# Three products of split operands for the local q, k and v in a two-branch transformer kernel

## Time and profile before

| | |
|---|---|
| median of 3 runs | 3817.17 us (3813.94 to 3817.77) |
| profiled execution | 3824.69 us, its span 3822.8 us |
| mean granted TensorE clock | 0.966 |
| TensorE busy | 3278.0 us, 86% |
| VectorE, ScalarE, GpSimd busy | 55%, 44%, 26% |

### The profile page before, as it was taken

How to read it: one execution, slowest core, us unless ns; L and a number is a source line. 1 busy time by engine, 2 the same in 40 slices (tenths; PEclk the granted TensorE clock), 3 DMA queues, 4 the chain that set the end, 5 groups by cost and what they waited for, 6 DMA issues and landing times.

```text
span 3822.8 us, 96024 instructions
## 1 busy us (share of the span) xinstructions
PE 3278.0 (86%) x35300; PEld 2174.9 (57%) x35300; DVE 2101.3 (55%) x7233; ACT 1694.2 (44%) x3181; POOL 983.3 (26%) x743
## 2 busy tenths in 40 slices
PE   1689898898989889898988989889898988979898
PEld 0356465565656556465655646566565655656565
DVE  2365564646556464654647556464655646465464
ACT  1245354444535354453544535344453534445354
POOL 2141230403223041321404133140412304132140
PEclk9799999999999999999999999999999999999999
DMA  3000000000000000000000000000000000000000
GB/s 79 1 7 2 10 2 10 2 2 10 2 10 2 10 2 2 10 2 10 2 5 7 2 10 2 10 2 2 10 2 10 2 10 2 2 7 2 7 2 4
DMA packets 42627, 26.49 MB, mean 7 GB/s; under 512 B 13266, under 2 KB 40828, under 8 KB 42108
## 3 DMA queue, kind: packets, MB, share of 16 engines
q1 hardware_dynamic: 42108, 19.59, 1.8%
HBM read 14.96 MB, written 4.19 MB: 5 GB/s over the span
## 4 chain that ended last, share of the span: by engine, by line
issue 43%; PE 28%; DVE 16%; POOL 6%; ACT 4%; SPq 1%; DMA 0%; DVEq 0%; POOLq 0%; ACTq 0%; PEldq 0%
PE bank L1093 4%; PE bank L1179 3%; DVE ss L925 3%; PE bank L1136 3%; POOL rnorm L652 3%; DVE scratch L920 3%; PE bank L1011 3%; PE bank L1122 2%; PE bank L1194 2%; DVE scratch L922 2%; DVE bank L865 2%; ACT scratch L757 2%; DVE scratch L923 2%; PE bank L1114 1%; DVE bank L880 1%
## 5 line engine op out<-in xcount | busy, mean ns | idle before, releaser
L652 POOL TENSOR_TENSOR rnorm<-ssc,minus_half 128x8 f32<-128x8 f32 x264 | 484.7, 1836 | 997.1 <-DVE ssc L927 994.6
L865 DVE CUSTOM_DVE_ANT_0 bank<-bank,future 128x128 f32<-128x128 f32 (+3 forms) x1024 | 467.0, 527 | 145.6 <-PE bank L1055 143.6
L880 DVE CUSTOM_DVE_ANT_0 bank<-bank,band 128x192 f32<-128x192 f32 x1056 | 341.3, 394 | 277.2 <-PE bank L1074 265.7
L723 ACT ACTIVATE probs<-bank 128x512 f32<-128x512 f32 (+1 forms) x768 | 347.0, 530 | 205.4 <-PE bank L1101 205.2
L1093 PE MATMUL bank<-Qa,Ka 64*128 64x512 f32 (+3 forms) x2048 | 395.1, 465 | 44.5 <-DVE ss L925 36.5
L1136 PEld LDWEIGHTS bank<-Va,probs 128*64 128x64 f32 x10240 | 338.8, 144 | 117.2 <-issue 107.4
L757 ACT ACTIVATE scratch<-bank 128x512 f32<-128x512 f32 x264 | 158.7, 601 | 512.0 <-DVE ss L925 286.1
L1136 PE MATMUL bank<-Va,probs 128*64 128x65 f32 x10240 | 375.2, 231 | 0.7
L641 POOL TENSOR_TENSOR lrstd<-lvar,minus_half 128x4 f32<-128x4 f32 x33 | 33.4, 1013 | 1308.1 <-DVE lvar L943 1308.1
L1179 PE MATMUL bank<-Lqkv,resid 128*128 128x512 f32 x528 | 289.2, 674 | 32.6 <-ACT resid L746 23.5
L731 ACT ACTIVATE lprobs<-bank 128x384 f32<-128x384 f32 x528 | 226.8, 491 | 199.0 <-PE bank L1124 195.5
(11 more groups left out here) (144 smaller groups left out, 7148.9 us busy)
## 6 DMA issues: line engine op xcount, KB each, us to landing
x_res<-in_L_attn_x SPq DMA_DIRECT2D x16, 256.0 KB, 2.9
x_rows<-in_L_attn_x SPq DMA_DIRECT2D x16, 256.0 KB, 3.1
out<-yT SPq DMA_DIRECT2D x16, 256.0 KB, 2.7
Lqkv<-in_L_ffn_wqkv SPq DMA_DIRECT2D x2, 768.0 KB
yT<-in_L_attn_W_qkv SPq DMA_DIRECT2D x6, 256.0 KB, 2.7
rope_t<-in_rope SPq DMA_DIRECT2D x8, 128.0 KB
Lw<-in_L_ffn_w SPq DMA_DIRECT2D x2, 341.0 KB
Lwo<-in_L_ffn_wo SPq DMA_DIRECT2D x2, 256.0 KB
```

The source lines that it names most:

```text
L652: g.tensor_tensor(rnorm[s][:, :], ssc[s][:, :], minus_half[:, :], ALU.pow).then_inc(rnorm_ready.sem, 1)
L723: psum.raise_read(a.activation(probs[j][:, at:at + n], psum.bank(task, (u, j))[:, 0:n], ACT.Exp, scale=float(HEAD) ** -0.5), task, (u, j))
L865: ins = v.tensor_tensor_reduce(psum.bank(task, (u, j))[:, at:at + n], psum.bank(task, (u, j))[:, at:at + n], future[:, SEQ - n:SEQ], 1.0, ...
L880: ins = v.tensor_tensor_reduce(psum.bank(task, (u, j))[:, k * BAND:(k + 1) * BAND], psum.bank(task, (u, j))[:, k * BAND:(k + 1) * BAND], b ...
```

## The change

The weights `Lqkv[l]` become a pair of a high and a low part, made once at the start. A new step `f_split` per layer makes the same pair `hT` of the layer's input (ScalarE copies the high part, VectorE subtracts), and `f_qk` and `f_v` use `product` with it. `h` goes away: the norm writes over `x_res`, and so SP loads `x_res` later, after the transposes `xt`, and behind the load of `x_rows`. The loads of all four weight thirds or halves that are split go to tiles that the loop uses later (`ff`, `GLU`, `Kf[1]`, `Qf[1]`), without a wait between them. The mask image `outside` loses an unused third. The planner has the new step, its needs, and new prices for `f_qk` and `f_v`, and so it gives a new order.

In the new order `a_neg.0` stands ahead of `f_qk.0.0`; `f_st.0.0` stands ten steps behind `f_neg.0.0`; the end of a turn reads `a_pv.7.1, f_ot.1.3, a_ot.7, f_wo.1, a_out.7, a_end, xt, f_down.0, f_mean.1, f_var.1, f_rep.1, f_gate.1, f_up.1.*, f_down.1, out`. Before it read `f_wo.1, a_out.6, a_pv.7.0, f_down.0, a_pv.7.1, f_mean.1, a_ot.7, f_var.1, a_out.7, a_end, xt, f_rep.1, f_gate.1, f_up.1.*, f_down.1, out`.

```diff
-    "f_qk": (0.9, [("act", 1.2, 0.0), ("dve", 5.2, 0.6), ("pool", 7.0, 2.9)], 2),
-    "f_v": (0.45, [("act", 0.6, 0.0)], 1),
+    "f_split": (0.0, [("act", 0.65, 0.0), ("dve", 0.7, 0.65)], 0),
+    "f_qk": (1.45, [("act", 1.2, 0.0), ("dve", 5.2, 0.6), ("pool", 7.0, 2.9)], 2),
+    "f_v": (0.72, [("act", 0.6, 0.0)], 1),
...
-    return start + [(kind, l, t) for kind, t in F_FRONT] + rounds(F_ROUND, LPAIRS, (l,)) + [("f_wo", l)]
+    return start + [("f_split", l)] + [(kind, l, t) for kind, t in F_FRONT] + rounds(F_ROUND, LPAIRS, (l,)) + [("f_wo", l)]
...
-        "f_qk": lambda: [("f_qk", 0, TILES - 1)] if at[0] else [("f_first",)],
-        "f_v": lambda: [] if at[0] else [("f_first",)],
+        "f_split": lambda: [("f_qk", 0, TILES - 1), ("f_v", 0, TILES - 1)] if at[0] else [("f_first",)],
+        "f_qk": lambda: [("f_split", at[0])],
+        "f_v": lambda: [("f_split", at[0])],
...
-        Lqkv = [sb(f"Lqkv{l}", [P, 3 * INNER]) for l in range(DEPTH)]
+        Lqkv = [[sb(f"Lqkv{l}_{s}", [P, 3 * INNER], F32R) for s in ("hi", "lo")] for l in range(DEPTH)]
-        outside = sb("outside", [P, 2, 3, BAND], BF16)
+        outside = sb("outside", [P, 2, 2 * BAND], BF16)
-        h = sb("h", [P, TILES, DIM])
+        hT = [sb(f"hT_{s}", [P, SEQ], F32R) for s in ("hi", "lo")]
...
+        PIECE = 3 * INNER
+        raw = [sem(f"raw{k}") for k in range(DEPTH + 2)]
+        staging = [part[:, 0:3].rearrange("p c n -> p (c n)") for part in (ff, GLU, Kf[1], Qf[1])]
+        split_parts = [(raw[k], staging[k][:, n * SEQ:(n + 1) * SEQ], [part[:, at + n * SEQ:at + (n + 1) * SEQ] for part in w])
+                       for k, (w, at) in enumerate([(Lqkv[0], 0), (Lqkv[1], 0), (Wqkv, 0), (Wqkv, PIECE)]) for n in range(PIECE // SEQ)]
...
-            for k in range(WPIECES):
-                if k:
-                    sp.wait_ge(split_lo, k)
-                sp.dma_start(yT[:, :], W_qkv[:, k * SEQ:(k + 1) * SEQ]).then_inc(staged, 16)
+            for k, part in enumerate(staging[DEPTH:]):
+                sp.dma_start(part, W_qkv[:, k * PIECE:(k + 1) * PIECE]).then_inc(raw[DEPTH + k], 16)
...
-                sp.wait_ge(norm_ready.sem, norm_ready.now(i, ("norm",), "n"))
+                psum.wait_read(sp, i, ("out",), "t", True)
+                sp.sem_inc(carried["sp"], 1)
+                load(x_rows[:, :, :], bass.ds(i, 1), x_again)
+                psum.wait_filled(sp, i, ("xt",), "x")
                 sp.sem_inc(carried["sp"], 1)
                 if last:
                     sp.sem_inc(x_loaded, 16)
                 else:
                     load(x_res[:, :, :], bass.ds(i + 2, 1), x_loaded)
-                psum.wait_read(sp, i, ("out",), "t", True)
-                sp.sem_inc(carried["sp"], 1)
-                load(x_rows[:, :, :], bass.ds(i, 1), x_again)
...
+                    elif kind == "f_split":
+                        l = task[1]
+                        if l == 0:
+                            psum.wait_read(act, i, ("f_first",), "h")
+                        else:
+                            psum.wait_read(act, i, ("f_down", 0), "w", True)
+                        act.sem_inc(carried["act"], 1)
+                        psum.wait_filled(act, i, ("f_v", 1 - l, TILES - 1), "v", l == 0)
+                        act.sem_inc(carried["act"], 1)
+                        a.activation(hT[0][:, :], resid[l][:, 0:SEQ], ACT.Copy).then_inc(hi_ready.sem, 1)
...
-                    ins = v.tensor_scalar(h[:, t, :], src[:, t, :], mv[:, t, 0:1], rstd[:, t:t + 1],
+                    ins = v.tensor_scalar(src[:, t, :], src[:, t, :], mv[:, t, 0:1], rstd[:, t:t + 1],
...
+                    elif kind == "f_split":
+                        l = task[1]
+                        dve.wait_ge(hi_ready.sem, hi_ready.now(i, task, "h"))
+                        v.tensor_tensor(hT[1][:, :], resid[l][:, 0:SEQ], hT[0][:, :].bitcast(F32),
+                                        ALU.subtract).then_inc(lo_ready.sem, 1)
...
-                            psum.raise_filled(mm(bank[:, :], resid[l][:, tile(t)], Lqkv[l][:, c * INNER:(c + 1) * INNER], start=True,
-                                                 stop=True), task, m)
+                            psum.raise_filled(product(bank[:, :], [part[:, tile(t)] for part in hT],
+                                                      [w[:, c * INNER:(c + 1) * INNER] for w in Lqkv[l]]), task, m)
```

More of the change, by code:

```diff
@@ L212, in in_order @@
     return at == sorted(at)
-assert in_order(("norm",), ("f_first",), ("f_qk", 1, 0), ("f_wo", 0), ("f_wo", 1), ("f_down", 0), ("f_mean", 1), ("out",))
+assert in_order(("norm",), ("f_first",), ("f_split", 1), ("f_qk", 1, 0), ("f_wo", 0), ("f_wo", 1), ("f_down", 0), ("f_mean", 1), ("out",))
 assert in_order(("norm",), ("f_first",), ("xt",)) and in_order(("a_proj", PAIRS - 1), ("xt",))
@@ L481, in prenorm_attention_and_local_transformer @@
         clip_ready = Signal(sem("clip_ready"), dict(f_qk="qk"))
+        hi_ready = Signal(sem("hi_ready"), dict(f_split="h"))
+        lo_ready = Signal(sem("lo_ready"), dict(f_split="l"))
         norm_ready = Signal(sem("norm_ready"), dict(norm="saen"))
@@ L557, in _ @@
                         sp.dma_start(dst[rows, k, :], src[of, :]).then_inc(halved, 16)
[L558 removed]
+                    sp.dma_start(outside[rows, k, :], band[of, 1:3, :].rearrange("p a n -> p (a n)")).then_inc(halved, 16)
             weights(1)
[L560 to L563 removed]
+            for k, part in enumerate(staging[DEPTH:]):
+                sp.dma_start(part, W_qkv[:, k * PIECE:(k + 1) * PIECE]).then_inc(raw[DEPTH + k], 16)
             sp.dma_start(Wout[:, :, :], W_out.rearrange("(c p) n -> p c n", p=P)).then_inc(whole[1], 16)
             sp.sem_inc(stored, 16)
[L566 removed]
+            psum.wait_filled(sp, -1, ("xt",), "x")
             load(x_res[:, :, :], slice(1, 2), x_loaded)
             def sequence(i, last):
[L571 removed]
+                psum.wait_read(sp, i, ("out",), "t", True)
+                sp.sem_inc(carried["sp"], 1)
+                load(x_rows[:, :, :], bass.ds(i, 1), x_again)
+                psum.wait_filled(sp, i, ("xt",), "x")
                 sp.sem_inc(carried["sp"], 1)
@@ L672, in _ @@
             act.wait_ge(params, PARAMS)
-            for k in range(WPIECES):
-                act.wait_ge(staged, 16 * (k + 1))
-                a.activation(Wqkv[0][:, k * SEQ:(k + 1) * SEQ], yT[:, :], ACT.Copy).then_inc(split_hi, 1)
+            for loaded, src, (hi, lo) in split_parts:
+                act.wait_ge(loaded, 16)
+                a.activation(hi, src, ACT.Copy).then_inc(split_hi, 1)
+            act.wait_ge(split_lo, len(split_parts))
             def alone(i, task, mark, dst, src, func=ACT.Copy, **kw):
@@ L809, in _ @@
                                     scales[:, l, kind:kind + 1, :].broadcast_to([P, TILES, HEAD]), ALU.mult).then_inc(tables, 1)
-            for k in range(WPIECES):
+            for k, (loaded, src, (hi, lo)) in enumerate(split_parts):
                 dve.wait_ge(split_hi, k + 1)
                 dve.sem_inc(carried["dve"], 1)
[L813 to L816, removed]
+                dve.wait_ge(loaded, 16)
+                v.tensor_tensor(lo, src, hi.bitcast(F32), ALU.subtract).then_inc(split_lo, 1)
+            dve.wait_ge(split_lo, len(split_parts))
             dve.wait_ge(tables, 4 * DEPTH)
@@ L1000, in _ @@
             pe.wait_ge(whole[0], WHOLE[0])
+            pe.wait_ge(split_lo, 3 * INNER // SEQ)
             def product(dst, left, right):
@@ L1025, in steps @@
                         pe.wait_ge(norm_ready.sem, norm_ready.now(i, ("norm",), "n"))
-                        transposes(i, task, "x", lambda t: h[:, t, :])
+                        transposes(i, task, "x", lambda t: x_res[:, t, :])
                     elif kind == "a_proj":
@@ L1114, in steps @@
                                     mm(bank[j][:, 0:2 * BAND], row_of[HALF[j], k, :],
-                                       outside[HALF[j], k, 1:3, :].rearrange("p a n -> p (a n)"), start=(k == 0), stop=False)
+                                       outside[HALF[j], k, :], start=(k == 0), stop=False)
                             for k in range(2):
@@ L1167, in steps @@
                         pe.wait_ge(norm_ready.sem, norm_ready.now(i, ("norm",), "n"))
-                        transposes(i, task, "h", lambda t: h[:, t, :])
+                        transposes(i, task, "h", lambda t: x_res[:, t, :])
                     elif kind == "f_qk":
@@ L1171, in steps @@
                         if t == 0:
-                            if l == 0:
-                                psum.wait_read(pe, i, ("f_first",), "h")
-                            else:
-                                psum.wait_read(pe, i, ("f_down", 0), "w", True)
+                            pe.wait_ge(lo_ready.sem, lo_ready.now(i, ("f_split", l), "l"))
                             pe.sem_inc(carried["pe"], 1)
@@ L1183, in steps @@
                         bank = psum.claim(pe, i, task, "v")
```

(6 more changed lines are left out.)

12 lines of the change are left out of this document (5 added, 7 removed).

## The result

The changed kernel takes 3916.4 us (median of 4 runs, 3910.6 to 3922.0) against 3817.0 of the kernel before (3813.9 to 3817.8): ratio 1.026, interval 1.024 to 1.027. It is slower, as predicted, but by 99 us and not 33; 3916 lies outside the range of 3770 to 3905. The profiled execution has a span of 3920.1 us and a mean granted clock of 0.928, before 3822.8 and 0.966.

What follows compares the result with a forecast made beforehand. TensorE's queue, 86% busy, was taken as the bound. A turn: -3.3 products, +0.7 middle, +1.3 head, +4.5 tail = +3.2; sixteen turns +51, start -18, so +33 us: 3850, range 3770 to 3905.

Steps and rivals of the forecast that it cites:

- The products' passes: q, k, v products as three passes each instead of float32: gain of 3.3 us a turn, ends 2.6 and 4.1.
- rival (c): q, k, v passes cost three quarters of the old, 2.1 us a turn better: 3816, no change; chance 0.11.
- The middle: Middle of the turn: bank waits grow, other waits go in the new order; +0.7 us a turn, ends -3 and +4.
- the count: TensorE work missing between a k product and the seventh bank after, per tile: total 8.9 to 12.6 us a turn.
- The head: Start of a turn: f_split.0's copy and subtraction in series delay f_qk.0.0; +1.3 us a turn, ends 0 and 2.6.
- The tail: f_down.0 to f_gate.1 with no other work left between: 3.8 us a turn bare, up to 7.1 with clock; 4.5 taken.
- the three new waits: Sign in the tail: waits of 1.2 to 1.6 us ahead of f_mean.1, f_var.1 and f_rep.1, sixteen of each.
- The clock: Lower clock priced only in the tail, between 3.8 and 7.1 us a turn; no clock term for head or middle.
- rival (b): Tail runs at the low clock as in the first sequence, 7.1 instead of 4.5 us a turn: 3892; chance 0.16.
- first pass: First layer-0 pass, ahead of the loop: f_split adds 1.4, four product pairs give back about 0.5 each; -0.6 us.
- The start: W_qkv loads issued at once ahead of the first norm, which moves from 66.2 to near 49: gain of 17 us.
- Rival (a): Steps moved from the tail cover the middle's waits, -3 there, -2.0 us a turn in all: 3767; chance 0.28.

Runs made afterwards that it cites:

- e11: Changed kernel in the old order, without the split step (q, k, v from wrong tokens), plus 33 zero-weight products a turn: 3785.0 us, ratio 0.991.
- e9: Kernel before with only the new loading of W_qkv at the start, plus 33 zero-weight products a turn ahead of eight waiting steps: 3791.9 us, ratio 0.993.
- e3: Changed kernel with the last steps of a turn in the old order, other work again between the tail's steps: 3870.7 us, ratio 1.014.
- e5: Changed kernel with three unused bf16 products added at each of five waits of the tail: 3936.3 us, ratio 1.030.
- e8: Changed kernel with 38 zero-weight products a turn ahead of ten waiting steps of the head and middle: 3868.0 us, ratio 1.012.
- e4: Kernel before with only the start changed, both halves of W_qkv loaded at once to tiles not used yet: 3803.5 us, ratio 0.996.
- e7: Kernel before with only the split step added, awaited by TensorE, products still float32: 3886.2 us, ratio 1.018.

## Why the prediction was half right

**The products' passes: right, at the upper end.** Timeline after, q, k and v of one tile at full clock:

```profile
1175.79 0.50 PE L1025 MATMUL bank<-Lqkv_hi,hT_hi 128*128 128x512 f32 x1
...
1177.29 0.39 PE L1025 MATMUL bank<-Lqkv_hi,hT_hi 128*128 128x512 f32 x1
...
1177.98 0.60 PE L1032 MATMUL bank<-ident,qn 128*128 128x128 f32 x4
```

Start to start: 1.50 for the pair, 0.69 for v, 2.19 a tile against 2.68. Times eight that is 3.9 us a turn, forecast 3.3 with an end at 4.1; that half of what lay between the ends was waiting for weight loads no run shows. Where v stands apart from its pair the tile gains a little less (1.50 and 0.80 against 1.82 and 0.91). The ratio is 0.82; the three quarters of rival (c) are out.

**The middle: the waits were right, their reading was the failure's first half.** Waits of TensorE after, the largest of the loop (the first line holds the head's, 2.25 us a turn ahead of `a_neg.0`):

```profile
PE bank L1103 <- DVE neg L880: 59.1, 48, 2.5
PE bank L1093 <- DVE ss L940: 53.8, 32, 1.9
PE bank L1095 <- DVE ss L940: 38.8, 16, 2.4
PE bank L1076 <- DVE ss L940: 38.3, 16, 2.8
```

Of the earlier trace rows the wait for negfT (39.9) is gone from the large ones, and the claim of 45.9 has 38.3. Beside it stand new bank waits of the sizes that the count gave: 38.3 / 16 = 2.4 (2.9 counted), 38.8 / 16 = 2.4 (2.5), and 53.8 / 32 = 1.7 (1.0 and 1.6). One tile's turning and reducing does limit when its bank comes back, whatever the product costs, and e11 beside e9 fits it: of the products' 3.9 us, 2.7 came back as waits.

**The head: right.** Timeline after, the head of a turn whose norm starts at 1128.3:

```profile
1135.04 0.63 ACT L775 ACTIVATE hT_hi<-resid 128x512 fp32r<-128x512 f32 x1 [0.27 <-ACT resid L754]
1135.70 0.69 DVE L952 TENSOR_TENSOR hT_lo<-resid,hT_hi 128x512 fp32r<-128x512 f32 x1
1135.79 0.61 PE L1103 MATMUL bank<-identb,neg 128*128 128x128 bf16 x4 [2.25 <-DVE neg L880]
1136.54 0.77 PE L1025 MATMUL bank<-Lqkv_hi,hT_hi 128*128 128x512 f32 x1
```

The copy and the subtraction run as worked out; `f_qk.0.0` starts 8.2 us behind the norm, before 6.7 (1107.98 of the earlier trace rows; that turn's norm starts at 1101.3): +1.5, less what its products save, against +1.3. The wait shows under another name: the row of `a_neg.0` ahead of it has 2.25, and `hT_lo` is not named.

**The tail: right in sum, by other parts.** Timeline after, `f_down.0` to `f_gate.1`:

```profile
1335.16 2.74 PE L1246 MATMUL bank<-GLU,Lw 128*128 128x512 f32 x6
1337.74 1.02 PE L1218 MATMUL bank<-resid,center 128*128 128x512 f32 x2
1339.94 1.05 PE L1222 MATMUL bank<-mean_of,ff 128*128 128x2 f32 x8 [1.17 <-ACT ff L799]
1342.42 1.75 PE L1229 MATMUL bank<-ident,lrstd 128*128 128x128 f32 x8 [1.43 <-POOL lrstd L648]
1345.76 4.72 PE L1236 MATMUL bank<-lT,Lw 128*128 128x512 f32 x6 [1.59 <-ACT lT L806]
```

Two of the three new waits are there (1.17 and 1.43). The third, ahead of `f_mean.1`, is not: `f_down.0` now stands between `f_wo.1` and it and covers its input. From the step behind `f_down.0` to `f_gate.1` it is 8.0, so 8.0 - 8.95 + 3.55 = +2.6, forecast 3.8. But `f_gate.1` runs at half clock, 4.6 us from its first start to `f_up`'s, before 2.7: +1.9, and it is 4.6 to 5.2 in all sixteen turns. Together 4.5, the value taken, with more clock in it than the 0.7 that I had put there. e3 gets 3.4 of it back.

**The clock: this step failed.** The sum had no term for the clock of the head and the middle; it was put at nothing, and measured 83 us. I priced the lower clock only behind the bare tail, as a choice between 3.8 and 7.1, and rival (b) likewise. At equal clock a turn costs +1.7 more than before; the forecast, whose tail had 0.7 us of clock in it (4.5 for 3.8), was +3.2. The mean over all turns is +6.9, and the 83 us between come from eleven turns that have longer stretches at half clock in the head, and others at 71, 108 and 149 us. The bank waits that I had counted one by one were read as time lost, and not as pauses after which the clock can drop. Rival (b)'s 3892 is near in number and wrong in place: the tail at half clock is there, and holding `f_gate.1` at full clock by fillers left the total where it was (e5), while filling the head and middle gave 48 us (e8). The page "TensorE: Matmul & The Clock Gate" of the Trainium skill (HAM oscillation) looks for one long gap; the trace again does not agree, since the clock drops behind waits of 1.91 and 2.42 us, and none in the loop is longer than 2.8. The next section of that page of the Trainium skill (A second HAM failure mode: psum-queue depth-cycling) has short pauses between groups of matmuls do the same, and with that the trace agrees.

At equal clock the change comes to 27 in the loop, 18 less at the start and 6 more in the first pass, +15 us, worked out and not run. So the sign of the forecast would have held without the slow turns. For what it priced, though, +33 was too high, and that this error points toward the measured 99 is luck.

A sum of terms could not give the combined effect either: order alone +90, split step alone +69, products with the start +28, all together +99. That they share the cost of the clock is the likely reason, and not shown for all of it.

**The start: right within a microsecond, its first pass wrong.** The first norm stands at 48.5, 17.7 us earlier against the forecast 17:

```profile
46.43 1.89 DVE L832 TENSOR_TENSOR Wqkv_lo<-Qf,Wqkv_hi 128x512 fp32r<-128x512 f32 x3
48.50 0.87 DVE L842 BATCH_NORM_STATS2 stats<-x_res 128x6 f32<-128x128 f32 x4 [0.17 <-DVE Wqkv_lo L832]
```

The first pass took 5.9 us more where I had -0.6. It has 65.5 us at half clock, before 51.7; at 0.29 that is 4.0 of the 6.5 between them, worked out and not tested. The start alone is worth 13.5 us (e4).

**Rival (a)** is out: the waits of the middle did not dissolve, idle went from 25.8 to 29.3.

**What stays open.** Why a turn falls into one kind or the other. Before, too, one turn with 10 us at half clock takes 225.3 and others with 20 to 23 take 228 to 230.6. The last turns of the changed kernel alternate nearly one for one. The waits of the middle are the same in both kinds, so something else decides; no run separates that. The kernel before has a wait of 2.4 us, too, 69 us into the turn (for `negfT`), and behind it only two of its sixteen turns drop. So it is also open why the change, and which of its pauses, brings the drops so often.

## What to carry to other kernels

Before you price a new order of a kernel that TensorE bounds, add up the time its clock stands at the lower level, turn by turn, and say what the change does to it: here 26 us more of it went with 7.5 us in a turn, and all waits and savings of the change together cost 1.7. Add it up by stretch as well, since a total that stays can hide one stretch that was cured and another that got worse (e5). Identical turns of different length are the sign to look for, and a few products with zero weights ahead of the waiting steps are a cheap test, here also a remedy (3803.5 to 3791.9). A shorter product behind a ring of banks is worth little while its bank is freed by another engine, and a serial step on two other engines in front of it cost more than its own length here (0.63 and 0.69 us, 1.5 at the head, 3.8 in the whole turn of e7).

## What the runs showed of the hardware

- Products with zero weights hold the granted clock up: 33 of 512 bf16 columns a turn of 226 us brought half-clock time from 11.9 to 3.8 us a turn (e4, e9).
- The granted clock fell to 1.2 GHz behind single waits of 1.91 and 2.42 us in eleven turns of the changed kernel, and stayed at 2.4 GHz behind the same waits in the other five.
- Turns with the same instructions in the same order took 235.7 and 228.2 us, with 39.6 and 13.2 us at 1.2 GHz.
- A float32 product of 512 columns took 0.86 to 0.91 us from start to start, three `F32R` products of the same size 0.69 to 0.80.
